# An attention layer in one kernel: joins in their own PSUM banks, two score slots, the query mask on TensorE, denominators inside the solve

## What is computed

```python
q, k = _rope(q, k)
s = einsum('bihd,bjhd->bhij', k, k) * scale      # strict lower triangle, softmax over j
p = e / where(denom == 0, 1.0, denom)
L = p * beta.transpose(0, 2, 1)[..., None]
A = L + eye(T)
u = solve_triangular(A, v.transpose(0, 2, 1, 3), lower=True)
sc = einsum('bihd,bjhd->bhij', q, k) * scale     # causal, softmax over j
attn = softmax(where(causal, sc, -inf))
o = einsum('bhij,bhjd->bihd', attn, u)
return o @ Wo
```

## Time and profile before

| | |
|---|---|
| median of the runs | 1285.95 us |
| profiled execution, its own time | 1298.2 us |
| its span, first to last instruction | 1296.3 us |
| TensorE busy | 798.2 us, 62% |
| VectorE busy | 571.6 us, 44% |
| ScalarE busy | 284.9 us, 22% |
| GpSimd busy | 267.6 us, 21% |
| granted TensorE clock, mean | 0.721 |

### The profile page before, as it was taken

One profiled execution on the slowest core, in us unless ns is written; L12 is line 12 of the kernel. 1 busy time (PEld: TensorE's weight loads), 2 busy tenths in 40 slices (PEclk: granted clock), 3 DMA queues, 4 the chain that ended last, 5 costly groups with the idle time before them and its releaser, 6 DMA issues. The chain is left out here.

```text
span 1296.3 us, 16178 instructions
## 1 busy us (share of the span) xinstructions
PE 798.2 (62%) x5790; PEld 529.6 (41%) x5791; DVE 571.6 (44%) x1556; ACT 284.9 (22%) x429; POOL 267.6 (21%) x305
## 2 busy tenths in 40 slices
PE   5376077767775777577400299999704055199990
PEld 3232045425542553354300288888602025066660
DVE  4276955395449546721550033333334554033232
ACT  1012030432054215413100133333200221011110
POOL 4001010150025002401077400000077300400005
PEclk9688555755577558658555599999956576599995
DMA  3607000530054017000592478878433100211113
GB/s 118 86 14 112 21 2 2 156 49 2 2 155 50 1 44 312 10 33 1 171 402 104 148 260 261 282 268 270 147 99 101 53 1 1 81 41 40 49 36 101
DMA packets 71262, 132.50 MB, mean 102 GB/s; under 512 B 11424, under 2 KB 35360, under 8 KB 70176
## 3 DMA queue, kind: packets, MB, share of 16 engines
q1 hardware_dynamic: 59168, 96.92, 25.6%
q0 software_dynamic: 7680, 20.98, 5.0%
q10 hardware_dynamic: 4352, 13.77, 2.7%
HBM read 77.18 MB, written 54.26 MB: 101 GB/s over the span
## 5 line engine op out<-in xcount | busy, mean ns | idle before, releaser
L879 POOL TENSOR_SCALAR_AFFINE_SELECT E<-E 128x256 f32<-128x256 f32 x128 | 78.9, 641 | 419.5 <-ACT E L782 419.4
L588 DVE TENSOR_REDUCE block_maxima<-scores 128x10 f32<-128x1280 f32 x64 | 94.7, 1490 | 103.4 <-PE scores L320 103.3
L1064 PE MATMUL scores<-xgT,wgu 128*96 128x256 f32 x512 | 121.5, 380 | 0.0
L1254 POOL DMA_INDIRECT gb<-expert_outputs,gather_slots x64 | 65.2, 1019 | 223.4 <-SPq L1247 204.2
L1133 DVE TENSOR_TENSOR hT<-sg,scores 96x256 f32<-96x256 f32 x64 | 26.7, 418 | 184.9 <-ACT sg L1170 184.9
L782 ACT ACTIVATE E<-scores 128x1280 f32<-128x1280 f32 x64 | 77.3, 1237 | 92.7 <-PE scores L331 92.3
L1041 PE MATMUL misc<-cf,xg 128*128 128x128 f32 x256 | 39.4, 277 | 93.5 <-DMA xg<-expert_rows 93.5
L1064 PEld LDWEIGHTS scores<-xgT,wgu 128*96 128x96 f32 x512 | 80.3, 164 | 20.8 <-issue 0.2
L1493 PE MATMUL scores<-w,xgT 128*128 x184 | 87.8, 601 | 0.3 <-issue 0.3
L1181 POOL DMA_INDIRECT expert_rows<-xn_moe,scatter_slots x64 | 62.5, 977 | 69.8 <-DVE gather_slots L1110 50.6
L320 PE MATMUL scores<-cb 128*128 128x128 bf16 x256 | 76.9, 303 | 0.0
(11 more groups left out here) (220 smaller groups left out, 1437.2 us busy)
## 6 DMA issues: line engine op xcount, KB each, us to landing
expert_rows<-zero SPq DMA_DIRECT2D x32, 512.0 KB, 6.1
xg<-expert_rows SPq DMA_DIRECT2D x64, 256.0 KB, 4.2
expert_outputs<-yb SPq DMA_DIRECT2D x64, 256.0 KB, 3.8
wgu<-in_wgu SPq DMA_DIRECT2D x32, 384.0 KB, 3.3
w<-in_w ACTq DMA_DIRECT2D x8, 1024.0 KB
wd<-in_wd SPq DMA_DIRECT2D x32, 192.0 KB, 3.6
w<-in_w ACTq DMA_DIRECT2D x8, 512.0 KB
split_heads<-E SPq DMA_DIRECT2D x8, 384.0 KB, 2.5
```

Of the source, the lines that this page charges most:

```text
L588: nc.vector.tensor_reduce(bm[:, c, h, :], scores[:, slot, 0:WIDE].rearrange("p (a n) -> p a n", n=P), AX.X, ALU.max).then_inc(s_fd, 1)
L879: ins = nc.gpsimd.affine_select(out=d, in_=d, pattern=[[0, 2], [1, P]], base=0, channel_multiplier=-1, compare_op=ALU.is_ge if c else ALU. ...
L1064: ins = nc.tensor.matmul(scores[0:F0, j % 2, g * CAP:(g + 1) * CAP], wgu[:, j // GE, j % GE, k, g * F0:(g + 1) * F0], xgT[:, j % 2, k, :], ...
L1254: pool.indirect_dma_start(out=gb[:, g % NG, :], out_offset=None, in_=ybuf, in_offset=bass.IndirectOffsetOnAxis(ap=ig[:, t, k:k + 1], axis= ...
```

## The change

Five things are edited. The joins write to the banks of `misc` instead of slot 1, so both score slots serve the next unit's row scores in turn, and the turned maxima go to the unused end of a score slot; the joins of a unit now wait for the last unit's `ao_ready`. The query mask becomes a matmul of the mask with the identity on TensorE, and GpSimd keeps only the key heads. In the solve, the key heads are issued earlier (0, 1, 2 in the first block) and the denominators stand ahead of the last block's transposes; VectorE gathers the blocks ahead of its last copy of U. The parts have eight buffers, so the wait for a store is gone. `project(2)` stands ahead of a wait.

```diff
 ropes = early[:, 2048:3072].rearrange("p (a n) -> p a n", a=2)
-parts = early[:, 3072:4608].bitcast(BF16).rearrange("p (a b n) -> p a b n", a=2, b=3)
-wvb = early[:, 4608:5152].rearrange("p (k n) -> p k n", k=KT)
+parts = early[:, 3072:9216].bitcast(BF16).rearrange("p (a b n) -> p a b n", a=8, b=3)
+wvb = early[:, 9216:9760].rearrange("p (k n) -> p k n", k=KT)
 wo0 = EE[:, 0, 0, 0:KT * D].rearrange("p (k n) -> p k n", k=KT)
...
     q.dma_start(scr[c, :, hg * P:(hg + 1) * P, b * T:(b + 1) * T].rearrange("t p n -> p t n"),
-                parts[:, w % 2]).then_inc(s_pw[w % 2], 16)
+                parts[:, w]).then_inc(s_pw[w % 2], 16)
...
             pe.wait_ge(s_nms, 2 * u + c + 1)
-            if u >= 2:
-                pe.wait_ge(s_ao, 2 * (u - 1))
-            nc.tensor.transpose(misc[0:96, c, 0:64].bitcast(BF16),
+            pe.wait_ge(s_fd, 16 * u + (9 if u and not c else 16))
+            nc.tensor.transpose(scores[0:96, c, WIDE:WIDE + 64].bitcast(BF16),
                                 nms[:, c, :, :].rearrange("p a b -> p (a b)"), identb
...
                                        stk["kq"[c]][0:KR + 3, u % 2, h, jt * P:T],
-                                       start=True, stop=True)
+                                       start=True, stop=not c)
+                if c:
+                    ins = nc.tensor.matmul(scores[:, k % 2, o:o + P], mask["q", jt], identb,
+                                           start=False, stop=True)
             ins.then_inc(s_sc, 1)
...
                 if li == 1:
-                    ins = nc.tensor.matmul(scores[64:128, 1, 64 * h:64 * h + 64], e[0:64, 64:128],
+                    ins = nc.tensor.matmul(misc[64:128, 0, 64 * h:64 * h + 64], e[0:64, 64:128],
                                            XR[0:64, x, :], start=True, stop=True)
...
                 if li == 1:
-                    ins = nc.tensor.matmul(scores[0:64, 1, 1024 + 64 * h:1088 + 64 * h], T1[64:128, q % 2, h, :],
+                    ins = nc.tensor.matmul(misc[0:64, 1, 64 * h:64 * h + 64], T1[64:128, q % 2, h, :],
                                            XT[64:128, x, 64:128], start=True, stop=True)
...
                     if not last:
-                        key_scores(u + 1, [2 * it])
+                        key_scores(u + 1, [2 * it + 1])
                     pe.wait_ge(s_sn, 3 * u + it)
...
                 if not last:
-                    key_scores(u + 1, [2 * it + 1] if it else [0, 1])
+                    if it < NI - 1:
+                        key_scores(u + 1, [2 * it + 2] if it else [0, 1, 2])
+                    else:
+                        denominators(u + 1)
                 pe.wait_ge(s_un, 4 * u + it + 1)
...
 
-            pe.wait_ge(s_dq, GH * u + 4 * (hh + 1))
+            pe.wait_ge(s_fa, use(1, u) + 4 * (hh + 1))
             for jt in range(NI):
...
         turn_maxima(0, 1)
-        pe.wait_ge(s_mr, 2)
         project(2)
+        pe.wait_ge(s_mr, 2)
         key_scores(0, [0, 1])
...
                 pe.wait_ge(s_fa, use(1, u - 1) + GH)
+                pe.wait_ge(s_ao, 2 * u)
             else:
...
                         stacks_loaded(u + 1)
-                    for m in maxima_due(q):
-                        pe.wait_ge(s_fd, 16 * (u + 1) + m)
-                        row_scores(u + 1, m, 0)
                     if q == 5:
                         turn_maxima(u + 1, 0)
+                    for m in maxima_due(q):
+                        if m >= 2:
+                            pe.wait_ge(s_fd, 16 * (u + 1) + m - 1)
+                        if m == 10:
+                            pe.wait_ge(s_mr, 2 * u + 3)
+                        row_scores(u + 1, m, m % 2)
             join(u, 7)
...
                 pe.wait_ge(s_mr, 2 * u + 4)
-            elif u:
-                pe.wait_ge(s_ao, 2 * u)
             pe.wait_ge(s_lv, 8 * (u + 1))
             solve(u)
-            if not last:
-                denominators(u + 1)
             pe.wait_ge(s_ml[1], 48 * (u + 1))
...
             dve.wait_ge(s_pj, w + 1)
-            if w >= 2:
-                dve.wait_ge(s_pw[w % 2], 16 * (w // 2))
             a0, a1 = ropes[:, 0, :], ropes[:, 1, :]
...
                 nc.vector.tensor_copy(bankT[:, 256:512], misc[:, 1, 0:256]).then_inc(s_un, 1)
+                if it == NI - 1 and u + 1 < UNITS:
+                    gather_blocks(u + 1)
                 dve.wait_ge(s_ut, 4 * u + it + 1)
...
                     for m in maxima_due(q):
-                        maxima(u + 1, m, 0)
+                        maxima(u + 1, m, m % 2)
             solved(u)
             if not last:
-                gather_blocks(u + 1)
                 scale(u + 1)
...
 
-        def select(u, c):
+        def select(u):
 
             for h in range(GH):
-                pool.wait_ge(s_fa, use(c, u) + h + 1)
+                pool.wait_ge(s_fa, use(0, u) + h + 1)
                 e = Eu(u)[:, h, :]
...
 
-        select(0, 0)
-        pool.wait_ge(s_dk, GH)
         for u in range(UNITS):
+            select(u)
+            pool.wait_ge(s_dk, GH * (u + 1))
             fill_XR(u)
-            if u + 1 < UNITS:
-                select(u + 1, 0)
-            select(u, 1)
-            pool.wait_ge(s_dq, GH * (u + 1))
```

More of the change, by code:

```diff
@@ L381, in sums @@
                             for lo, hi in PAIRS:
-                                ins = nc.tensor.matmul(scores[hi, 1, 32 * h:32 * h + 32], e[lo, hi], LB[lo, :, x],
+                                ins = nc.tensor.matmul(misc[hi, 0, 32 * h:32 * h + 32], e[lo, hi], LB[lo, :, x],
                                                        start=True, stop=True, skip_group_check=True,
@@ L693, in scaled_sums @@
                             ins = nc.vector.tensor_tensor(
-                                T1[hi, q % 2, :, 0:n], scores[hi, 1, 0:GH * n].rearrange("p (h n) -> p h n", h=GH),
+                                T1[hi, q % 2, :, 0:n], misc[hi, 0, 0:GH * n].rearrange("p (h n) -> p h n", h=GH),
                                 g_[hi].to_broadcast([hi.stop - hi.start, GH, n]), ALU.mult)
@@ L776, in rows @@
                             act.wait_ge(s_ml[c], 48 * u)
-                        nc.scalar.copy(mrow[:, c, :], misc[0:96, c, 0:64].bitcast(BF16)).then_inc(s_mr, 1)
+                        nc.scalar.copy(mrow[:, c, :], scores[0:96, c, WIDE:WIDE + 64].bitcast(BF16)).then_inc(s_mr, 1)
                     def exps(u, c, h):
```

26 lines of the change are left out of this document (13 added, 13 removed).

## The result

| | before | changed |
|---|---|---|
| median of the runs | 1285.28 us (1283.23 to 1292.17) | 1225.52 us (1215.23 to 1232.09) |
| profiled execution, its own time | 1298.2 us | 1232.1 us |
| its span | 1296.3 us | 1230.4 us |
| granted TensorE clock, mean | 0.721 | 0.735 |

The ratio is 0.952, with a 95% interval of 0.944 to 0.960: faster, and forecast was 1229, a ratio of 0.956. A second comparison with the same kernel gave 1220.8 against 1286.0, ratio 0.949 (0.946 to 0.952), an interval that leaves the forecast just outside. Its runs spread over 16.9 and 13.8 us in the two comparisons, where those of before spread over 8.9 and 5.6; a clock that is not the same in each execution turns out to be the main finding.

What follows compares the result with a forecast made beforehand. No engine was taken to bound the whole kernel: waits inside stages are the time, each stage with its own bound. Six terms sum to -56.6 us, from 1285.95 to 1229 us, range 1199 to 1248.

Steps and rivals of the forecast that it cites:

- Two slots: Joins: row scores no longer wait for the previous head's reduction, 15.3 us less in each of three units, -45.9 us.
- term 2: Start of the joins in units 1 to 3: first sums wait for ao_ready, 3 x 1.2, +3.6 us.
- Masks: Inversions of units 1 to 3: 20.4 us instead of 23.3 without GpSimd's query masks, -8.7 us; last unit 0.
- Order of the solve: Solve to inversion: early key heads, denominators ahead of the last transposes; 0.3 us more in three units, +0.9 us.
- That move is free: End of the solve: VectorE's gather of the blocks ahead of its last copy of U costs nothing.
- Buffers and projection: Before unit 0's inversion: no store wait, 8.2 us, and projection 2 ahead of a wait, 0.3; -8.5 us.
- Stacks and outputs late: Stack loads for unit u + 2, or outputs, come late: 1 us in two units, +2.0 us (0 to +6).
- B: Rival: inversions stay at 23.3 us because exps, matmuls or DMA, not masks, slow VectorE; 1238 us, chance 0.13.
- C: Rival: first row scores of units 2 and 3 wait for stack loads; slower than before, chance 0.03.
- D: Rival: two slots bring little, VectorE arrives late with the joins' products; 1252 us, chance 0.09.
- A: Rival: TensorE's clock rises in the joins, VectorE bounds them at 39 us, 9.7 less per unit; 1200 us, chance 0.15.
- nearest row: Last unit's joins, TensorE busy 14.97 of 17 us at clock 0.50: taken as evidence for no clock rise.

Runs made afterwards that it cites:

- one_slot: Changed kernel with the next unit's row scores back in one score slot, joins still in misc: 1275.8 us, ratio 0.994.
- first_sums: Changed kernel with each unit's first sums written to slot 1 of scores, so they do not wait for ao_ready: 1218.9 us, ratio 0.948.
- masks_on_gpsimd: Changed kernel with the query masks back on GpSimd: 1230.2 us, ratio 0.957.
- slots_only: Kernel before with only both slots for row scores, joins in misc and maxima turned into scores: 1246.6 us, ratio 0.969.
- two_parts: Changed kernel with the parts in two buffers again, so VectorE waits for a store: 1221.5 us, ratio 0.949.
- old_solve_order: Changed kernel with the old order of key heads, denominators and VectorE's gather in the solve: 1227.9 us, ratio 0.955.
- bunched: Changed kernel with a unit's 16 row scores in four groups of four and the first maxima turned in step 6: ratio 0.952.
- fours_new: Changed kernel with first sums in slot 1, gather split 5 to 11, U's last copy later, row scores in steps 4, 1, 4, 1, 4, 1, 1: 1221.2 us, 0.941.

## Why the prediction was right, and where not

The number was right, and its closeness is in part luck. At the clock that the prediction assumed, which the first profile has in most of its joins, the stages gained 53.9 us, 3 less than forecast. The medians gained 59.8 and 65.2 us. The clock's rise in some of the joins of some executions, which the prediction had put at nothing, is what the second profile shows for it. Term by term:

1. **Two slots: -45.9.** The first profile has 49.2, 51.0, 51.1 where before has 64.8, 65.0, 65.0; with the 1.2 us of term 2 in two of them taken off, -46.0. `one_slot` shows the waits as the cause. What was left out is that the clock is not the same in each execution: in the second profile it is -57.5.
2. **Wait for `ao_ready`: +3.6.** 2.70 us against 1.45, three times: +3.7, and `first_sums` takes it back.
3. **Masks: -8.7.** Three times -3.0 with the turns: -9.0; `masks_on_gpsimd` gives it back in the same units. In the last unit the masks were put at 0. It took 3.5 us more, of which 1.2 are term 2 and 0.6 the solve, at 0.50 instead of 0.55. The rest is its query scores and outputs, from their first matmul on, 23.0 us where before has 21.3. Here they are in the kernel before, `slots_only` (both with GpSimd's masks), the changed kernel and `two_parts` (both with TensorE's):

```profile
584.52:605.82 21.30, 14.09 (x106) 5.63 (x103) 1.65 (x5) 10.61 (x10) 6.11 (x16) 0.84 0.00 1
545.54:569.25 23.71, 17.77 (x106) 6.63 (x103) 1.65 (x5) 10.63 (x10) 6.12 (x16) 0.64 0.00 1
528.86:551.88 23.02, 17.71 (x138) 9.26 (x135) 1.66 (x5) 10.66 (x10) 0.00 (x0) 0.72 0.00 1
533.22:553.71 20.49, 14.75 (x138) 7.68 (x135) 1.65 (x5) 10.47 (x10) 0.00 (x0) 0.92 0.00 1
```

The length goes with the clock, whichever engine masks (`masks_on_gpsimd`: 24.2 at 0.63). Between these points the masks on TensorE cost 0.3 us or less, an estimate, so the 0 was right and the 1.7 us are the clock's.
4. **Order of the solve: +0.9.** This step failed, in two ways that nearly cancel. "That move is free": it isn't, since denominators and gather now end in the other order, and from the denominators' copy to the inversion's first product it is 6.5 to 6.7 us where before has 5.1. And the denominators' price was taken as fixed; their start came 22.52 us behind the solve's, against 22.93, the 0.4 us of the prediction, but they ran in 4.51 us instead of 6.16, at the full clock. At like clock the sum is 1.4 - 1.65 - 0.4 = -0.6 us per unit (34.2 to 33.6 in unit 0), and `old_solve_order` says that the whole is no loss.
5. **Buffers and projection: -8.5.** -9.4 and -4.7 in the two profiles. The second one's first reduction came at 58.4 us, before's at 56.2, and the first one's at 55.9: counted from there it is -9.1 and -6.9. The difference that is left is mostly projection 7, 3.70 us at the full clock and 5.40 at a mean of 0.68. So the stage did about what the term says, but `two_parts` has the same ratio as the changed kernel, and the kernel's time does not show it.
6. **Stacks and outputs late: +2.0.** Nothing. The first row scores of units 2 and 3 start at 266.38 and 377.72, right behind TensorE's work before them, and the outputs were ready.

The sum by stages in the first profile: -9.4 - 43.6 + 4.6 - 9.0 + 3.5 = -53.9; in the second -4.7 - 55.1 + 0.8 - 9.0 + 3.5 = -64.5. The forecast, -56.6, lies between. The rivals: B, C and D are out (the earlier trace rows against `masks_on_gpsimd`; no wait for a stack; 1.4 us of waits). A had 0.15 and is true of some units in some executions, at a smaller price: 5.6 and 6.3 us in the two units of the second profile where the clock rose, not 9.7, for it rose in a part of the stage only. The prediction asked whether the clock rises in the joins, yes or no, and took the earlier trace rows as the nearest row. This is the step that failed beside term 4. It was the wrong row: the last unit's joins have no row scores, and in `bunched` and `fours_new` the clock rose where these stand four in a row. What it is in such a group that raises the clock was not taken apart. The Trainium skill, "TensorE: Matmul & The Clock Gate" (Part 1, on the clock gate), says that sustained activity releases the throttled clock; the runs agree with its direction, 0.50 to 0.53 with the row scores apart and 0.72 to 0.80 with four in a row, but a TensorE that was busy 46.92 of 49.50 us also stayed at 0.50.

## What to carry to other kernels

Where two engines hand one buffer to and fro, count the waits per round and the sum is good to a few per cent; what spoils it is a change of TensorE's clock, so state the time of a stage at both levels. If a kernel's runs spread far more than before, compare the granted clock of its stages in two profiles, then try the large matmuls in dense groups where the rest of the step still hides the other engines. A piece of work moved off the critical path is free only until the order of the two arrivals behind it turns round: look which comes last afterwards.

## What was not expected of the hardware

- The clock came back within joins that, at 0.50, had TensorE almost fully busy, for 17 us in one execution and not at all in another. Groups of four row scores did it in all six units of two profiles (0.68 to 0.80), alternating with small matmuls left the clock at 0.50 to 0.53 in all three units.
- GpSimd's masks make VectorE's 122 instructions take 2.9 us more, 23.3 against 20.4. The same masks as 128-column matmuls on TensorE cost the last unit 0.3 us or less, an estimate from stretches at clocks of 0.63 to 0.92.
- In an unedited layer ScalarE waited 27 to 28 us in some profiles and about 8 in the others, and all behind the attention layer was some 12 us longer with it. It came and went with the set of runs, whatever the kernel. Its cause is open.
